# First graph loop: ScalarE fetches a second tile of every twelfth superstep row by row

## Chip, cores and metric

One core of one Trainium2 chip runs the kernel. The metric is the device time of one execution in microseconds, as the median of the runs.

## What is computed

Two graph layers over 12500 nodes with 64 features and 200000 edges, sorted by destination. Each layer is followed by a residual and a layer norm. The reference, cut to what matters:

```python
# layer 0
all_feat = concat([x[dst], x[src], edge_attr, u_per_node[dst]])
msg = relu(all_feat @ W1 + b1)
agg = segment_sum(msg, dst, num_segments=12500)
x = layernorm(x + relu(concat([x, agg, u_per_node]) @ W2 + b2))
# layer 1: relational attention, 8 relations
Z = einsum('ni,rio->nro', x, fc_weight)
z_s, z_d = Z[src, etype], Z[dst, etype]
e = relu(sum(concat([z_s, z_d]) * attn_weight[etype]))
alpha = exp(e - segment_max(e)[dst]) / segment_sum(...)[dst]
x = layernorm(x + segment_sum(alpha * z_s, dst))
```

## The kernel before

**Tiling.** The edges lie in NT = 1563 tiles of 128 edges. O = 8 tiles make a superstep of the table, of which there are TO = 196. A tile whose edges go to two blocks of 128 nodes is worked on twice, so the consuming engines run SO = 208 supersteps of eight slots. Superstep s of the consumers needs the table up to a superstep that they read from a row of numbers (`xrow`); it is at most s + 1 supersteps and lags behind s more and more, 12 in the end.

**The first loop** (`phase_layer0`) adds up the messages of layer 0. In it,

- GpSimd (POOL) gathers: `gathers` issues one indirect DMA for each tile (line 522). It reads 128 rows of 64 floats of `Btab` (x[src] times its weights, made beforehand) into the tile `ring`. The ring has RT = 20 supersteps of the table, and three spare ones of eight tiles. At the first tile of superstep s >= 20 it waits for `full` of consumer superstep s - 20 + 13 (`BEHIND` = 13), and at tiles 2, 4 and 6 for sums before that. After the fourth tile of superstep s, `counted(s - 1)` (line 510) waits for the DMAs of superstep s - 1 and raises `landed` by one.
- SyncE (SP) issues for each consumer superstep the load of `eaT` (edge features, line 636), which waits for TensorE's count `c` (line 635), and every fourth the load `drow` (line 534). Beside it `fetched` (lines 476 to 496) fetches the last tile (j = 7) of every twelfth superstep of the table, 17, 29, ... (NK = 15 tiles), one row after another, by 128 small DMAs with a row number from a register. It spreads them over twelve consumer supersteps, 11 rows (`ROWS`) in each. `numbers` (line 473) loads the 128 row numbers of the next such tile. POOL leaves these 15 tiles out, and `counted` waits for their rows too (`s_row`). For k = 0 the rows are issued in consumer supersteps 0 to 11, and `counted(17)` asks for them.
- TensorE (PE) multiplies A3 by the one-hot `oht` (line 791), and `eaT` (line 796), and then sums the messages by destination (line 804).
- VectorE (DVE) makes the one-hot tiles (902, 906), adds the three parts (945), adds the gathered rows of `ring` (`full`, line 925, which waits for `landed`), then adds slot by slot into `p_t` (931), and adds the sums into `acc0` (918).
- ScalarE (ACT) does one thing in each of the 208 supersteps: it waits for `pre` and writes `msg` = relu of `p_t` (line 704). PE's sums of the superstep and DVE's next line 945 wait for it. Before the loop it zeroes `acc0` (line 701).

**Around it.** Each phase is a block that all engines end together. `phase_mid` computes x1 and `Ztab`, and `phase_layer1` is a second loop of the same shape with POOL gathering from `Ztab`, SP fetching 15 tiles by rows, and ACT busy with two sets of activations in each superstep. The edge source numbers come from `in_srcT_in`, or from `srcT_s` where the edges had to be sorted first; SP has one copy of its loop for each case.

Of the kernel before, what the change touches and what calls it, by code (L numbers as in the profile page):

```python
# [13 lines left out]
P = 128  # L14
# [44 lines left out]
class Chain:  # L59


    def __init__(self, e, sem):
        self.e, self.sem = e, sem
# [401 lines left out]
def fetched_tile(k):  # L465


    return (FIRST + k * W) * O + O - 1


def numbers(e, A, of, k):

    e.dma_start(A.srow[0:1, k % 2 * P:(k % 2 + 1) * P], of[:, fetched_tile(k):fetched_tile(k) + 1].rearrange("p c -> c p"),
                allow_slow_non_contiguous=True).then_inc(A.s_srow, 16)


def fetched(e, A, s, ring, table, of, regs, used):


    k, i = divmod(s, W)  # L480
    if k >= NK:
        return
    t = fetched_tile(k)
    if i == 0:
        if k >= 2:

            e.wait_ge(used, t // O - SPARE * W + BEHIND + 1)
            e.wait_ge(A.s_row[k % 2], 16 * P * (k // 2))
        e.wait_ge(A.s_srow, 16 * (k + 1))
        if k + 1 < NK:  # L490
            numbers(e, A, of, k + 1)
    for p in range(i * ROWS, min((i + 1) * ROWS, P)):
        if p % O == 0 or p == i * ROWS:
            e.reg_load(regs, A.srow[0:1, k % 2 * P + p // O * O:k % 2 * P + p // O * O + O])
        r = e.snap(regs[p % O], min_val=0, max_val=table.shape[0] - 1)
        e.dma_start(ring[p:p + 1, place(t), :], table[bass.ds(r, 1), :]).then_inc(A.s_row[k % 2], 16)


def gathers(e, A, ring, table, idx, s_g, landed, used, summed, free={}):

    others = {fetched_tile(k): k for k in range(NK)}
# [3 lines left out]
    def counted(s):  # L505
        e.wait_ge(s_g[s % len(s_g)], 16 * sum(tiles(i) for i in range(s % len(s_g), s + 1, len(s_g))))
        k = others.get(s * O + O - 1)
        if k is not None:
            e.wait_ge(A.s_row[k % 2], 16 * P * (k // 2 + 1))
        e.sem_inc(landed, 1)  # L510
# [27 lines left out]
def phase_layer0(nc, A):  # L538
# [3 lines left out]
    with ExitStack() as ctx:  # L542
# [51 lines left out]
        s_io = sem("l0_io")  # L594
        T = {n: sem("t_" + n) for n in ("dve count before middle low high typ val sq sel tab d0 rows rowt rowi table dh dl lt yt ys "
# [4 lines left out]
        def _(e):  # L600
# [21 lines left out]
            def loads(of, src):  # L622
                numbers(e, A, src, 0)
                for s in range(SO):
# [12 lines left out]
                    fetched(e, A, s, ring, A.Btab, src, regs, S["full"])  # L637
# [7 lines left out]
        @block.gpsimd  # L645
        def _(e):
            gathers(e, A, ring, A.Btab, idx, s_g, S["landed"], S["full"], S["acc"], {XT0 // O: (T["a"], len(CHUNKS))})

        @block.scalar
        def _(e):  # L650
# [50 lines left out]
            e.activation(A.acc0, A.ones[:, 0:D].unsqueeze(1).to_broadcast([P, NB + 1, D]), ACT.Copy, scale=0.0).then_inc(T["zero"], 1)  # L701
            for s in range(SO):
                e.wait_ge(S["pre"], s + 1)
                e.activation(msg[:, s % 2, :, :], pT[:, :, :], ACT.Relu).then_inc(S["msg"], 1)  # L704

# [254 lines left out]
def phase_mid(nc, A):  # L960
# [6 lines left out]
    with ExitStack() as ctx:  # L967
# [31 lines left out]
        s_zd = [sem(f"mid_zd{i}") for i in range(ZR)]  # L999
        s_ix = sem("mid_ix")  # L1000
# [302 lines left out]
def phase_layer1(nc, A):  # L1303

    QO, QT, QV = 5, 3, 4
    with ExitStack() as ctx:
# [39 lines left out]
        def _(e):  # L1346
            numbers(e, A, A.ix1_d, 0)
            regs = [e.alloc_register(f"l1sr{j}") for j in range(O)]
            for s in range(SO):
                if s % G == 0:  # L1350
                    rows_loaded(e, A, drow, s_dr, S["oht"], s // G)
                fetched(e, A, s, ring, A.Ztab, A.ix1_d, regs, S["s"])
            e.wait_ge(A.s_srow, 16 * NK)

        @block.gpsimd
        def _(e):
            gathers(e, A, ring, A.Ztab, idx, s_g, S["landed"], S["s"], S["acc"])
# [300 lines left out]
def build(nc, A):  # L1658
    with ExitStack() as ctx:
# [28 lines left out]
        A.srow = A.tabs[96:97, 0:2 * P]  # L1688

        A.s_row = [ctx.enter_context(nc.semaphore(f"rows_fetched{i}")) for i in range(2)]  # L1690
        A.s_srow = ctx.enter_context(nc.semaphore("row_numbers"))

# [91 lines left out]
```

## Time and profile before

| what | value |
|---|---|
| time, median of 3 runs | 5698.01 us (5693.83 to 5705.06) |
| span of the profiled execution | 4163.5 us |
| time less span | 1534.5 us |
| first loop, POOL's first gather to the end of the block | 36.1 to 2005.6 us of the span |
| PE, DVE, POOL busy | 78%, 72%, 72% of the span |
| ACT busy | 31% of the span |
| mean granted TensorE clock | 0.522 of full speed |

The profiled execution shows its span from the first to the last instruction, and no time of its own beside it, so the difference of 1534.5 us is between that span and the median of other executions. Busy shares don't count DMA issues, register work or waits: POOL at 72% can be at work without a break, since a gather's record covers only part of the distance to the next gather. `POOLq`, `SPq` and `ACTq` are the sequencers of these engines.

### The profile page before, as it was taken

The numbers are of one execution on the slowest core, as the hardware profiler recorded it, in microseconds if no ns is written. First come the engines' busy times: TensorE is split into PE (matmuls) and PEld (weight loads), VectorE is DVE, ScalarE is ACT, GpSimd is POOL, SyncE is SP. The second block draws the span as 40 slices with busy tenths as digits, with TensorE's granted clock in tenths as the row PEclk, the third lists the DMA queues.
The fourth block names the chain that finished last, engine by engine and source line by source line (L and its number), as shares of the span: only waits on it lengthen the run. The fifth ranks groups of instructions, "written<-read, shape, count | busy, mean of one in ns | idle before, by whom it ended". The sixth has DMA issues, their size and how long they took to land. (4 is left out here: it accounts for less than half of the span.)

```text
span 4163.5 us, 83378 instructions
## 1 busy us (share of the span) xinstructions
PE 3242.3 (78%) x17947; PEld 2881.6 (69%) x17947; DVE 2994.8 (72%) x9502; ACT 1276.9 (31%) x4180; POOL 3008.4 (72%) x3234
## 2 busy tenths in 40 slices
PE   7887777777777777777857787788888888888885
PEld 6776666676667676767637676777777777777774
DVE  6776676677777777777656666676767777777777
ACT  3000000000000000000334555455555555555555
POOL 5777777777777777777257777777777777777773
PEclk7555555555555555555675555555555555555555
DMA  5322222222222222222352122222222222222221
GB/s 185 104 74 71 72 61 72 70 73 62 72 72 73 72 73 62 75 69 63 140 211 60 49 59 60 60 60 49 59 60 52 56 59 51 58 59 69 49 59 38
DMA packets 183679, 300.98 MB, mean 72 GB/s; under 512 B 83240, under 2 KB 89756, under 8 KB 169885
## 3 DMA queue, kind: packets, MB, share of 16 engines
q1 hardware_dynamic: 82662, 189.29, 12.9%
q0 software_dynamic: 99072, 104.03, 11.9%
q8 instruction: 173, 2.83, 0.3%
q14 instruction: 310, 2.53, 0.2%
q10 hardware_dynamic: 1462, 2.30, 0.2%
HBM read 260.38 MB, written 34.99 MB: 71 GB/s over the span
## 5 line engine op out<-in xcount | busy, mean ns | idle before, releaser
L522 POOL DMA_INDIRECT ring<-Btab,idx x1548 | 1473.7, 952 | 505.0 <-issue 325.8
L522 POOL DMA_INDIRECT ring<-Ztab,idx x1548 | 1469.3, 949 | 481.3 <-issue 345.8
L1423 PE MATMUL p_s<-ring,ohx 128*128 x3328 | 809.8, 422 | 159.2 <-issue 156.6
L1423 PEld LDWEIGHTS p_s<-ring,ohx 128*128 128x128 f32 x3328 | 737.5, 326 | 179.3 <-issue 179.3
L804 PEld LDWEIGHTS p_s<-msg,oh 128*128 128x128 f32 x3328 | 726.0, 330 | 97.8 <-issue 97.6
L804 PE MATMUL p_s<-msg,oh 128*128 128x64 f32 x3328 | 756.6, 422 | 46.8 <-ACT msg L704 44.0
L791 PE MATMUL p_m<-A,oht 128*128 x1664 | 435.8, 364 | 394.1 <-DVE full L925 384.7
L704 ACT ACTIVATE msg<-p_t 128x512 f32<-128x512 f32 x208 | 124.2, 597 | 1786.6 <-DVE p_t L931 1786.6
L796 PE MATMUL p_m<-W1c,eaT 65*128 65x128 f32 x1664 | 574.3, 449 | 26.2 <-DMA eaT<-in_eaT_in 26.1
L791 PEld LDWEIGHTS p_m<-A,oht 128*128 128x128 bf16 x1664 | 233.2, 140 | 472.1 <-issue 426.0
L1511 DVE SCALAR_TENSOR_TENSOR XA<-XA,ff,p_s 128x65 f32 x1664 | 467.9, 281 | 127.7 <-DVE XA L1511 71.3
L1374 ACT ACTIVATE ohe<-oh,ev 128x128 f32<-128x128 bf16 x1664 | 505.1, 386 | 31.2 <-DVE ev L1471 31.2
L1368 ACT ACTIVATE ohx<-oh,ex 128x128 f32<-128x128 bf16 x1664 | 508.6, 388 | 0.0
L796 PEld LDWEIGHTS p_m<-W1c,eaT 65*128 65x128 f32 x1664 | 455.2, 334 | 37.0 <-DMA eaT<-in_eaT_in 30.9
L1402 PE MATMUL p_ei<-ring,ident_h 128*128 x1664 | 320.4, 197 | 193.5 <-POOLq L510 189.3
L925 DVE TENSOR_TENSOR full<-p_m,ring 128x512 f32 x208 | 143.4, 690 | 429.2 <-POOLq L510 415.7
L1408 PE MATMUL p_x<-ident,ohe 128*128 128x128 f32 x1664 | 397.5, 417 | 0.0
L931 DVE TENSOR_TENSOR p_t<-p_t,full 128x64 f32<-128x64 f32 x1664 | 386.1, 233 | 12.1 <-issue 6.6
L918 DVE TENSOR_TENSOR XA<-XA,p_s 128x64 f32 x1664 | 366.7, 220 | 35.5 <-issue 7.5
L945 DVE TENSOR_REDUCE p_t<-p_m 128x256 f32<-128x768 f32 x416 | 379.2, 954 | 17.2 <-PE p_m L796 16.6
L1402 PEld LDWEIGHTS p_ei<-ring,ident_h 128*128 128x128 bf16 x1664 | 173.3, 106 | 299.1 <-issue 228.4
L1481 DVE TENSOR_REDUCE mslot<-p_x 128x8 f32<-128x1024 f32 x208 | 254.7, 1224 | 160.6 <-PE p_x L1408 159.8
(225 smaller groups left out, 3114.3 us busy)
## 6 DMA issues: line engine op xcount, KB each, us to landing
drow<-drow_d SPq DMA_DIRECT2D x104, 1024.0 KB
ring<-Btab SPq DMA_DIRECT2D x1920, 0.2 KB
ring<-Ztab SPq DMA_DIRECT2D x1920, 0.3 KB
eaT<-in_eaT_in SPq DMA_DIRECT2D x208, 128.0 KB
Ztab<-Z_stage SPq DMA_DIRECT2D x49, 536.0 KB, 5.2
ring<-Btab,idx POOLq DMA_INDIRECT x1548
ring<-Ztab,idx POOLq DMA_INDIRECT x1548
xTB<-in_xTB_in SPq DMA_DIRECT2D x7, 448.0 KB, 7.7
```

Of the source, the lines that this page charges most:

```text
L522: e.indirect_dma_start(out=ring[:, place(t), :], out_offset=None, in_=table[:, :], in_offset=bass.IndirectOffsetOnAxis(ap=idx[:, t:t + 1], ...
L791: e.matmul(parts(j), OHT[:, s % 2, j, :], A.A3[:, bass.ds(b, 1), :].rearrange("p a c -> p (a c)"), start=True, stop=True)
L796: last = e.matmul(own(j // 2), eaT[:, s % QE, j // 2, :], A.W1c2[:, :], start=True, stop=True)
L804: last = e.matmul(pS[r % 2][:, j, :], OH[:, r % QO, j, :], msg[:, r % 2, j, :], start=True, stop=True)
L931: ins = e.tensor_tensor(out=pT[:, j:j + 1, :], in0=pT[:, j:j + 1, :], in1=full[:, bass.ds(t, 1), :], op=ALU.add)
L945: e.tensor_reduce(out=pT[:, h * H:(h + 1) * H, :], in_=half(h), axis=AXX, op=ALU.add).then_inc(T["dve"], 1)
L1368: ins = e.activation(OHx[:, o, j, :], OH[:, s % QO, j, :], ACT.Copy, scale=ex[:, o, j:j + 1])
L1374: ins = e.activation(OHe[:, s % 2, j, :], OH[:, s % QO, j, :], ACT.Relu, scale=ev[:, s % QV, j:j + 1])
L1402: last = e.matmul(pE[:, j, :], A.ident_h[:, :], part.unsqueeze(2).to_broadcast([P, 3, R]), start=False, stop=True)
L1408: last = e.transpose(pX[:, j, :], OHe[:, s % 2, j, :], A.ident[:, :])
L1423: last = e.matmul(pS[s % 2][h][:, j % 4, :], OHx[:, s % 2, j, :], ring[:, bass.ds(t, 1), 0:D + 1], start=True, stop=True)
L1511: e.scalar_tensor_tensor(out=acc, in0=acc, scalar=ff[:, s % QV, j:j + 1], in1=pS[s % 2][j // 4][:, j % 4:j % 4 + 1, :], op0=ALU.mult, op1= ...
```

## The change

`fetched_tile` becomes a class `Rows` that holds which tile of the twelfth superstep is meant (`back`), where its numbers lie and its semaphores. SP keeps its tile (j = 7). In the first loop alone ACT gets a second one (`by_act`, `back` = 2, that is j = 6 of supersteps 17, 29, ...): after each relu it issues 11 row DMAs, with its own semaphores and numbers. Before its loop it writes the source numbers to a new array `srcT_d` and loads the first 128 numbers from there, so that it needs one copy of the loop alone. POOL leaves both tiles out, 30 in all where it left out 15, and `counted` waits for both. At its end ACT takes its semaphores back to zero, and `phase_mid` uses them again. The second loop stays with SP alone.

```diff
--- before.py
+++ after.py
@@ -462,51 +462,57 @@
     return RING + n % SPARE * O + j if off == 0 and n >= 0 else t % RING
 
 
-def fetched_tile(k):
-
-
-    return (FIRST + k * W) * O + O - 1
-
-
-def numbers(e, A, of, k):
-
-    e.dma_start(A.srow[0:1, k % 2 * P:(k % 2 + 1) * P], of[:, fetched_tile(k):fetched_tile(k) + 1].rearrange("p c -> c p"),
-                allow_slow_non_contiguous=True).then_inc(A.s_srow, 16)
-
-
-def fetched(e, A, s, ring, table, of, regs, used):
+class Rows:
+
+
+    def __init__(self, back, numbers, s_numbers, s_rows, before=0):
+        self.back, self.numbers, self.s_numbers, self.s_rows, self.before = back, numbers, s_numbers, s_rows, before
+
+    def tile(self, k):
+        return (FIRST + k * W) * O + O - self.back
+
+
+def numbers(e, rows, of, k):
+
+    t = rows.tile(k)
+    e.dma_start(rows.numbers[0:1, k % 2 * P:(k % 2 + 1) * P], of[:, t:t + 1].rearrange("p c -> c p"),
+                allow_slow_non_contiguous=True).then_inc(rows.s_numbers, 16)
+
+
+def fetched(e, rows, s, ring, table, of, regs, used):
 
 
     k, i = divmod(s, W)
     if k >= NK:
         return
-    t = fetched_tile(k)
+    t = rows.tile(k)
     if i == 0:
         if k >= 2:
 
             e.wait_ge(used, t // O - SPARE * W + BEHIND + 1)
-            e.wait_ge(A.s_row[k % 2], 16 * P * (k // 2))
-        e.wait_ge(A.s_srow, 16 * (k + 1))
+            e.wait_ge(rows.s_rows[k % 2], 16 * P * (k // 2))
+        e.wait_ge(rows.s_numbers, 16 * (k + 1 + rows.before))
         if k + 1 < NK:
-            numbers(e, A, of, k + 1)
+            numbers(e, rows, of, k + 1)
     for p in range(i * ROWS, min((i + 1) * ROWS, P)):
         if p % O == 0 or p == i * ROWS:
-            e.reg_load(regs, A.srow[0:1, k % 2 * P + p // O * O:k % 2 * P + p // O * O + O])
+            e.reg_load(regs, rows.numbers[0:1, k % 2 * P + p // O * O:k % 2 * P + p // O * O + O])
         r = e.snap(regs[p % O], min_val=0, max_val=table.shape[0] - 1)
-        e.dma_start(ring[p:p + 1, place(t), :], table[bass.ds(r, 1), :]).then_inc(A.s_row[k % 2], 16)
-
-
-def gathers(e, A, ring, table, idx, s_g, landed, used, summed, free={}):
-
-    others = {fetched_tile(k): k for k in range(NK)}
+        e.dma_start(ring[p:p + 1, place(t), :], table[bass.ds(r, 1), :]).then_inc(rows.s_rows[k % 2], 16)
+
+
+def gathers(e, A, ring, table, idx, s_g, landed, used, summed, fetchers, free={}):
+
+    others = {rows.tile(k) for rows in fetchers for k in range(NK)}
     tiles = lambda s: sum(t < NT and t not in others for t in range(s * O, (s + 1) * O))
 
 
     def counted(s):
         e.wait_ge(s_g[s % len(s_g)], 16 * sum(tiles(i) for i in range(s % len(s_g), s + 1, len(s_g))))
-        k = others.get(s * O + O - 1)
-        if k is not None:
-            e.wait_ge(A.s_row[k % 2], 16 * P * (k // 2 + 1))
+        k, off = divmod(s - FIRST, W)
+        if off == 0 and 0 <= k < NK:
+            for rows in fetchers:
+                e.wait_ge(rows.s_rows[k % 2], 16 * P * (k // 2 + 1))
         e.sem_inc(landed, 1)
 
     for t in range(NT):
@@ -592,6 +598,7 @@
         s_ea = [sem(f"l0_ea{q}") for q in range(QE)]
         s_dr = [sem(f"l0_dr{q}") for q in range(2)]
         s_io = sem("l0_io")
+        by_act = Rows(2, A.arow, A.s_arow, A.s_arows, 1)
         T = {n: sem("t_" + n) for n in ("dve count before middle low high typ val sq sel tab d0 rows rowt rowi table dh dl lt yt ys "
                                         "drow typd ix a hi lo rem parts zero").split()}
         block = ctx.enter_context(nc.Block())
@@ -620,7 +627,7 @@
             rows_loaded(e, A, drow, s_dr, S["oht"], 0)
 
             def loads(of, src):
-                numbers(e, A, src, 0)
+                numbers(e, A.by_sp, src, 0)
                 for s in range(SO):
                     if s == 4:
 
@@ -634,7 +641,7 @@
                         e.wait_ge(S["c"], s - QE + 1)
                     t = e.snap(treg, min_val=1, max_val=TO)
                     e.dma_start(eaT[0:2 * DE, s % QE, :, :], of[bass.ds(t, 1), :, :, :].rearrange("a f i k -> (a f) i k")).then_inc(s_ea[s % QE], 16)
-                    fetched(e, A, s, ring, A.Btab, src, regs, S["full"])
+                    fetched(e, A.by_sp, s, ring, A.Btab, src, regs, S["full"])
 
             bad = descends(e, A, "l0_sp")
             with e.If(bad == 0):
@@ -644,7 +651,7 @@
 
         @block.gpsimd
         def _(e):
-            gathers(e, A, ring, A.Btab, idx, s_g, S["landed"], S["full"], S["acc"], {XT0 // O: (T["a"], len(CHUNKS))})
+            gathers(e, A, ring, A.Btab, idx, s_g, S["landed"], S["full"], S["acc"], [A.by_sp, by_act], {XT0 // O: (T["a"], len(CHUNKS))})
 
         @block.scalar
         def _(e):
@@ -699,9 +706,20 @@
             e.wait_ge(T["drow"], 16)
             e.wait_ge(T["typd"], 32)
             e.activation(A.acc0, A.ones[:, 0:D].unsqueeze(1).to_broadcast([P, NB + 1, D]), ACT.Copy, scale=0.0).then_inc(T["zero"], 1)
+            e.dma_start(A.srcT_d, idx[:, :]).then_inc(A.s_arow, 16)
+
+            regs = [e.alloc_register(f"l0ar{j}") for j in range(O)]
+
+            e.wait_ge(A.s_arow, 16)
+            numbers(e, by_act, A.srcT_d, 0)
             for s in range(SO):
                 e.wait_ge(S["pre"], s + 1)
                 e.activation(msg[:, s % 2, :, :], pT[:, :, :], ACT.Relu).then_inc(S["msg"], 1)
+                fetched(e, by_act, s, ring, A.Btab, A.srcT_d, regs, S["full"])
+
+            for k in range(2):
+                take(e, A.s_arows[k], 16 * P * len(range(k, NK, 2)))
+            take(e, A.s_arow, 16 * (NK + 1))
 
         @block.tensor
         def _(e):
@@ -996,8 +1014,8 @@
             "b2 turned copied w2 o1 ln sub sq var root x1").split())
         s_ps, s_se, s_pp, s_zp, s_z, s_zv, s_za, s_cont, s_v = (sem("mid_" + n) for n in (
             "s s_copied parts zparts z zv za cont pool").split())
-        s_zd = [sem(f"mid_zd{i}") for i in range(ZR)]
-        s_ix = sem("mid_ix")
+        s_zd = A.s_arows + [sem(f"mid_zd{i}") for i in range(2, ZR)]
+        s_ix = A.s_arow
         block = ctx.enter_context(nc.Block())
         Zv = A.Ztab.rearrange("(b p r) c -> p b (r c)", p=P, r=R)
         blocks = lambda i: slice(i * LNB, (i + 1) * LNB)
@@ -1344,17 +1362,17 @@
 
         @block.sync
         def _(e):
-            numbers(e, A, A.ix1_d, 0)
+            numbers(e, A.by_sp, A.ix1_d, 0)
             regs = [e.alloc_register(f"l1sr{j}") for j in range(O)]
             for s in range(SO):
                 if s % G == 0:
                     rows_loaded(e, A, drow, s_dr, S["oht"], s // G)
-                fetched(e, A, s, ring, A.Ztab, A.ix1_d, regs, S["s"])
+                fetched(e, A.by_sp, s, ring, A.Ztab, A.ix1_d, regs, S["s"])
             e.wait_ge(A.s_srow, 16 * NK)
 
         @block.gpsimd
         def _(e):
-            gathers(e, A, ring, A.Ztab, idx, s_g, S["landed"], S["s"], S["acc"])
+            gathers(e, A, ring, A.Ztab, idx, s_g, S["landed"], S["s"], S["acc"], [A.by_sp])
 
         @block.scalar
         def _(e):
@@ -1686,9 +1704,14 @@
         A.wrow = A.tabs[32:33, :].rearrange("a (s j) -> a s j", j=O)
         A.xrow = A.tabs[64:65, 0:SO * WX].rearrange("a (s w) -> a s w", w=WX)
         A.srow = A.tabs[96:97, 0:2 * P]
+        A.arow = A.tabs[96:97, 2 * P:4 * P]
 
         A.s_row = [ctx.enter_context(nc.semaphore(f"rows_fetched{i}")) for i in range(2)]
         A.s_srow = ctx.enter_context(nc.semaphore("row_numbers"))
+        A.by_sp = Rows(1, A.srow, A.s_srow, A.s_row)
+
+        A.s_arows = [ctx.enter_context(nc.semaphore(f"act_rows{i}")) for i in range(2)]
+        A.s_arow = ctx.enter_context(nc.semaphore("act_row_numbers"))
 
         A.dstl = sb("dstl", [P, NS], BF16)
 
@@ -1769,6 +1792,7 @@
     A.typ_s = dr("typ_s", (SCP * P,), I32)
     A.srcT_s = dr("srcT_s", (P, NTP), I32)
     A.typT_s = dr("typT_s", (P, NTP), I32)
+    A.srcT_d = dr("srcT_d", (P, NTP), I32)
     A.ea_s = dr("ea_s", (EP, DE), F32)
     A.eaT_s = dr("eaT_s", (TO + 1, 2 * DE, O // 2, P), F32)
     A.drow_d = dr("drow_d", (NS, P), BF16)
```

## Rows read from the trace of the kernel before

**Rows 1.** The page: the span, and busy time, share and count of each engine.

```profile
span 4163.5 us, 83378 instructions
PE 3242.3 (78%) x17947; PEld 2881.6 (69%) x17947; DVE 2994.8 (72%) x9502; ACT 1276.9 (31%) x4180; POOL 3008.4 (72%) x3234
```

**Rows 2.** The page's costliest groups: busy, mean of one, idle before and its releaser.

```profile
L522 POOL DMA_INDIRECT ring<-Btab,idx x1548 | 1473.7, 952 | 505.0 <-issue 325.8
L704 ACT ACTIVATE msg<-p_t 128x512 f32<-128x512 f32 x208 | 124.2, 597 | 1786.6 <-DVE p_t L931 1786.6
L925 DVE TENSOR_TENSOR full<-p_m,ring 128x512 f32 x208 | 143.4, 690 | 429.2 <-POOLq L510 415.7
```

**Rows 3.** Windows of the loop, with and without SP's rows: length, then busy (xcount).

```profile
130.00:1730.00 1600.00, 1219.24 (x5572) 1101.89 (x5573) 1190.05 (x3644) 103.28 (x173) 1210.34 (x1279) 0.50 0.24 70
1760.00:1980.00 220.00, 167.66 (x769) 151.99 (x768) 164.53 (x505) 14.33 (x24) 166.50 (x176) 0.50 0.24 65
```

**Rows 4.** Timeline mid-loop: start, length, instruction, idle before and releaser.

```profile
...
1002.95 0.94 POOL L522 DMA_INDIRECT ring<-Btab,idx  x1 [0.30 <-issue]
...
1004.20 0.94 POOL L522 DMA_INDIRECT ring<-Btab,idx  x1 [0.30 <-issue]
...
1008.09 0.69 DVE L925 TENSOR_TENSOR full<-p_m,ring 128x512 f32 x1 [2.94 <-POOLq L510]
...
1011.86 0.60 ACT L704 ACTIVATE msg<-p_t 128x512 f32<-128x512 f32 x1 [9.35 <-DVE p_t L931]
...
1019.14 0.60 ACT L704 ACTIVATE msg<-p_t 128x512 f32<-128x512 f32 x1 [6.69 <-DVE p_t L931]
...
1026.03 0.60 ACT L704 ACTIVATE msg<-p_t 128x512 f32<-128x512 f32 x1 [6.29 <-DVE p_t L931]
...
```

**Rows 5.** Timeline at the start of the first loop, POOL and ACT.

```profile
...
36.13 1.13 POOL L522 DMA_INDIRECT ring<-Btab,idx  x1 [33.14 <-POOLq L309]
...
81.79 5.48 ACT L701 ACTIVATE XA<-ones 128x6336 f32<-128x6336 f32 x1
93.63 0.60 ACT L704 ACTIVATE msg<-p_t 128x512 f32<-128x512 f32 x1 [6.35 <-DVE p_t L931]
```

**Rows 6.** Timeline: relu of supersteps 11 and 13, gathers of tiles 147 and 160.

```profile
...
190.68 0.60 ACT L704 ACTIVATE msg<-p_t 128x512 f32<-128x512 f32 x1 [6.47 <-DVE p_t L931]
...
205.67 0.60 ACT L704 ACTIVATE msg<-p_t 128x512 f32<-128x512 f32 x1 [6.30 <-DVE p_t L931]
...
225.80 0.94 POOL L522 DMA_INDIRECT ring<-Btab,idx  x1 [0.30 <-issue]
...
242.03 0.94 POOL L522 DMA_INDIRECT ring<-Btab,idx  x1 [0.30 <-DVE full L925]
```

**Rows 7.** Timeline at the end of the first loop, POOL and ACT.

```profile
...
1980.68 0.94 POOL L522 DMA_INDIRECT ring<-Btab,idx  x1 [0.30 <-DVE XA L918]
...
1997.47 0.60 ACT L704 ACTIVATE msg<-p_t 128x512 f32<-128x512 f32 x1 [6.39 <-DVE p_t L931]
...
2005.56 0.27 POOL L1244 MEMSET Z_stage<- 128x96 f32 x1 [23.93 <-POOLq L542]
```

**Rows 8.** SP's own waits: who waited for whom, us in total, times, longest.

```profile
SPq L635 <- PEq L802: 506.5, 161, 11.0
```

**Rows 9.** Timeline of SP in supersteps 1 and 2.

```profile
...
90.47 0.53 SPq L636 DMA_DIRECT2D eaT<-in_eaT_in  x1
91.73 5.20 SPq L496 DMA_DIRECT2D ring<-Btab  x11
97.67 0.49 SPq L636 DMA_DIRECT2D eaT<-in_eaT_in  x1
```

**Rows 10.** Line 496, one row DMA: count, ns min/median/max.

```profile
...
L496 SPq DMA_DIRECT2D ring<-Btab x1920: 219/225/322, 84.4 to 1737.9; - x192
```

**Rows 11.** Timeline: the same kind of load issued by SP and by ACT.

```profile
...
2005.57 2.11 SPq L1277 DMA_DIRECT2D xT<-in_xTA_in  x4
...
2005.98 2.03 ACTq L1099 DMA_DIRECT2D xT<-in_xTA_in  x3
```


## Prediction

> **What bounds the kernel now.** I read the page first. Its span is 4163.5 us and no engine is busy for more than 78% of it [rows 1], so busy shares don't name the bound. The costliest groups do. For the first loop they show 1548 indirect gathers on POOL, a mean of 952 ns each, with 505.0 us idle before them, or 0.33 us each [rows 2]. Is that idle time a wait? In the timeline two gathers start at 1002.95 and 1004.20 us: 0.94 us of work and 0.30 us put down to "issue", which is the same before every gather [rows 4]. The table of windows says it for the whole loop: 1279 gathers in 1600 us, 1.251 us each (its columns are busy times, POOL's the last of the five, with the count in brackets) [rows 3]. POOL is never stopped; 505.0 less 1548 x 0.30 less the 33.1 us before the first gather [rows 2, 5] leaves nothing to speak of. Those who wait are the others: DVE's line 925 waits 415.7 us for POOL's sequencer, and ACT waits 1786.6 us of the loop for DVE [rows 2]. Where DVE has its rows already it makes a superstep in 1026.03 - 1019.14 = 6.89 us [rows 4]; POOL needs 1548 x 1.251 / 208 = 9.31 us for one on average. So **POOL's count of gathers sets the first loop**, from 36.1 us to its last gather at 1980.7, with 24.9 us behind it to the end of the block, which is the other engines' last supersteps at their own pace [rows 5, 7].
>
> **The sum.** POOL loses 15 gathers of 1.251 us: 15 x 1.251 = 18.8 us. Its waits stay: the change adds one in `counted`, 15 times, beside the one for SP's rows; the next gathers are queued behind it, and DVE waits for `landed`, so it matters only if ACT's rows are late (next paragraph). The end of the loop moves with POOL's last gather, since the supersteps behind it carry no row fetches (the 15 tiles are issued in supersteps 0 to 179 of 208) and keep their 24.9 us [rows 7]. `phase_mid` and the second loop only start earlier. The span becomes 4163.5 - 18.8 = 4144.7 us. The time of 5698.0 us has 1534.5 us around the span, which no row explains; I hold it constant: **5698.0 - 18.8 = 5679.2 us**.
>
> **Are ACT's rows in time for POOL?** For the first tile (superstep 17) ACT issues its last rows after the relu of superstep 11, at 190.7 us; `counted(17)` comes with the gather of tile 147 at 225.8 us, now 1.3 us earlier [rows 6]. Between them lie 34 us, for some 7 us of issuing and a landing. Later tiles have more: ACT's superstep 12k + 11 against POOL's 12k + 18, where both go at POOL's pace. The other wait of POOL, for `full` of superstep 13 at tile 160, is met about 205.7 us and asked for at 242.0 [rows 6]: 36 us for any slowing of DVE.
>
> **What ACT pays.** 1920 row DMAs, 195 or so register loads, 15 number loads. The trace has no such work on ACT; the nearest is SP's. SP goes from `eaT`'s issue to the next in 97.67 - 90.47 = 7.20 us; of that 5.20 us are 11 rows, 0.473 each, and 0.73 us lie between `eaT`'s end and the first row [rows 9]. With those prices ACT needs 0.60 + 0.73 + 5.20 = 6.5 us in a superstep, under even DVE's 6.89. ACT may issue more slowly: of the same kind of load SP issues four in 2.11 us, 0.53 each, and ACT three in 2.03, 0.68 each [rows 11]. A row at 0.473 x 0.68/0.53 = 0.61 us gives 0.60 + 0.73 + 6.7 = 8.0 us. That delays the relu in the short supersteps by 1.1 us, and with it PE's line 804 and DVE's 945, which wait for `msg`; but the mean superstep is still POOL's 1533 x 1.251 / 208 = 9.22 us, and the delay goes into DVE's wait for POOL. At the start of the loop it adds up over some 14 supersteps to 15 us, inside the 34 and 36 us above. So I cost it at nothing, between nothing and rival 1; a gain is excluded, as ACT's relu gets no earlier.
> From which price does it count? relu 0 is at 93.6, relu 207 at 1997.5 us [rows 5, 7], and the last 27 supersteps at 6.9 take 187 us, so supersteps 0 to 179 have 1717 us; less some 15 for the one stall among them (rival 1) it is 9.5 each. ACT reaches that at (9.5 - 1.33)/11 = 0.74 us a row, SP at 0.473 + (9.5 - 7.2)/11 = 0.68.
>
> **What comes before the loop.** ACT writes `srcT_d` (784 KB), waits for it, and loads 128 numbers. Zeroing `acc0` ends at 87.3 us and the first relu starts at 93.6, 6.35 us idle [rows 5]. If it doesn't fit, the first supersteps slip by a few us, and POOL, at work since 36.1 us, has the same 34 us of room.
>
> **The descriptor hardware.** A row DMA is recorded with 225 ns, under half of its 473 ns [rows 9, 10]. If only those 225 ns exclude the other queue, two streams need 450 ns of each 473 and both fit, barely. If each row waits in full for one of the other's, it costs 225 ns more. The Trainium skill speaks for the second: "Perfetto Trace Analysis", section on the HWDGE DMA instruction, says that the two sequencers share one descriptor generator, locked for exclusive use, and that the reported time includes the wait for the lock. By this rule the sum would be rival 1's. That two queues issue at once with 0.53 and 0.68 us a load [rows 11] shows no doubling.
>
> **The rivals.**
> 1. **SP becomes the bound, slower.** Place: SP's eleven rows, with the next `eaT` queued behind them, for which PE waits. Price: each row waits 0.225 us for one of ACT's, SP's superstep is 7.20 + 11 x 0.225 = 9.7 us. Then relu 207 comes at 93.6 + 180 x 9.7 + 187 + about 15 us (the stall in supersteps 3 and 4, where SP's queue holds the load of x) = 2042 instead of 1997.5: +44 us, 5742. It decides from 0.68 us a row on. For it: the 450 of 473 ns. Against it: SP today waits 506.5 us in the loop for PE [rows 8], which is 2.4 us a superstep, and ACT issues in only part of SP's time. Chance 9%.
> 2. **The gathers get dearer and nothing is gained.** 18.8 / 1533 = 0.012 us more for each gather, 1%, would eat it all: 5698. POOL writes its descriptors while ACT's transfers run. Against it: with SP's rows 1600/1279 = 1.251, without them 220/176 = 1.250 us [rows 3]; one stream of rows costs 1 ns at most. This case also holds that the fetched tiles don't lie where POOL is bound. Chance 10%.
> 3. **The time around the span grows with the program.** It is 1534.5 us over 83378 recorded instructions [rows 1], 18 ns each. The change adds at least 2 x 1920 and some for the registers, about 4100: +75 us, 5698 - 19 + 75 = 5754. No row supports a charge per instruction. Chance 5%.
> 4. **It shrinks with POOL's gathers.** 1534.5 / 3096 gathers = 0.50 us each, 15 x 0.50 = 7 us more saved: 5672. Chance 5%.
> The Trainium skill ("Runtime: NRT & Kernel Launch", its section on the preamble and postamble) gives a launch about 15 us; 1534.5 us here is a hundred times that, so the page doesn't explain it, and I take nothing from it.
>
> **How the numbers follow.** Forecast 71%, rivals 9, 10, 5 and 5%. The likeliest time is 5679.2. The runs shown lie 11 us apart, so a median may be off by some 4 us; the forecast alone is 5674 to 5685. The range takes in rival 4 (5672 less 4) and rival 2 (5698 and some): 5668 to 5702, and leaves out rivals 1 and 3, 14%. About 0.2%, or 11.4 us, is what a measurement of this kernel can tell from no change: faster means below 5686.6. The forecast is 7 us under that; of its 71% I give 66 to faster and 5 to same. Faster: 66 + 5 = 71%; same: 5 + 10 = 15%; slower: 14%.
>
> **What would show it.** In the trace after: 1533 gathers from `Btab`, still 1.25 us from start to start, and no new wait on POOL; POOL's last gather near 1962 us; the second loop as long as before. ACT's row DMAs at 0.47 to 0.61 us apart and its relu at least 6.5 us apart; SP's rows still near 0.47. The window without row fetches should look as before. I am wrong if SP's or ACT's rows stand over 0.7 us apart, if POOL's gathers start more than 1.26 us apart, if DVE's line 925 no longer waits for POOL, or if the span falls by 19 us and the time does not.

## The result, and the profile after

| | before | after | ratio, 95% interval |
|---|---|---|---|
| beside the timed runs shown ahead of the prediction | 5703.1 us (5693.8 to 5715.9) | 5769.9 us (5732.5 to 5785.9) | 1.0102 [1.0080, 1.0123] |
| on another chip (e5) | 4159.6 us (4152.5 to 4162.2) | 4140.0 us (4133.6 to 4144.9) | 0.9955 [0.9941, 0.9968] |

The forecast was 5679.2 us. The change made the kernel 1.0% slower where it was timed. On another chip it made the same kernel 0.45% faster. The kernel before takes 5.70 to 5.78 ms on some chips and 4.16 ms on others, always the same kind for all executions on one chip, and the trace shown ahead of the prediction (span 4163.5 us) is of the second kind while the times beside it are of the first.

The page of the changed kernel where it was timed. The rows with digits are busy tenths in 40 slices, PEclk is the granted TensorE clock; in the groups the columns are busy, mean ns, and idle before with its releaser. "issue" there means that the profile shows nothing the engine still waited for, "remote" that it can't name what raised the semaphore. The lines have moved: 528 is the gather (522 before), 717 the relu (704), 814 and 822 PE's `eaT` and its sums (796, 804), 936 DVE's sums into `acc0` (918), 943 `full` (925), 949 the additions into `p_t` (931), 963 the three parts (945).

```profile
...
span 5730.8 us, 89576 instructions
...
PE 3325.5 (58%) x17947; PEld 2864.8 (50%) x17947; DVE 3013.2 (53%) x9502; ACT 1277.1 (22%) x4180; POOL 2987.0 (52%) x3219
...
PE   4164544544454454555685076666666667666676
...
DVE  3264454545454455555684065555555555555567
...
POOL 4525555555555555555405616666666666666641
PEclk9999999999999999999997555555555555555555
...
L528 POOL DMA_INDIRECT ring<-Btab,idx x1533 | 1456.3, 950 | 1368.6 <-DVE XA L936 761.5
...
L814 PE MATMUL p_m<-W1c,eaT 65*128 65x128 f32 x1664 | 589.6, 458 | 735.2 <-DMA eaT<-in_eaT_in 641.3
...
L717 ACT ACTIVATE msg<-p_t 128x512 f32<-128x512 f32 x208 | 124.2, 597 | 2683.1 <-issue 1803.0
L963 DVE TENSOR_REDUCE p_t<-p_m 128x256 f32<-128x768 f32 x416 | 391.9, 962 | 613.1 <-remote 397.4
```

The span is 5730.8 us where [rows 1] had 4163.5, and that execution took 5732.5 us: 1.7 us around the span, not 1534.5. The first loop fills slices 2 to 21 (a slice is 143 us); from its first relu to its last are 2794 us, in place of 1904. POOL, without a break in [rows 2], has 1368.6 us of idle time before its gathers, 761.5 of it for DVE's sums, and its mean gather still takes 950 ns. PE waits 641.3 us for `eaT` from SP, ACT stands 2683.1 us. Nobody is the plain bound. Two of the prediction's signs of being wrong are there: DVE's line 943 no longer waits for POOL (before it, 200.3 us of "issue" and nothing else), and SP's rows stand 0.74 us apart at the median (0.42 in e5).

The same kernel on the other chip (e5), where the kernel before has the rows of the first trace again:

```profile
...
span 4134.9 us, 89576 instructions
...
PE 3230.8 (78%) x17947; PEld 2874.3 (70%) x17947; DVE 2995.2 (72%) x9502; ACT 1276.8 (31%) x4180; POOL 2987.8 (72%) x3219
...
L528 POOL DMA_INDIRECT ring<-Btab,idx x1533 | 1454.2, 949 | 501.1 <-issue 345.2
...
L717 ACT ACTIVATE msg<-p_t 128x512 f32<-128x512 f32 x208 | 124.2, 597 | 1768.9 <-DVE p_t L949 1747.9
...
L943 DVE TENSOR_TENSOR full<-p_m,ring 128x512 f32 x208 | 143.6, 690 | 408.4 <-POOLq L516 396.4
```

Here all reads as in [rows 1, 2]: 1533 gathers, 501.1 us idle before them, DVE waiting 396.4 us for POOL.

### The profile page after: what moved, and what is told of

Same layout as the page of the kernel before. It is cut to its first block and busy times, and to the rows that moved or that the text cites. A ratio compares the mean times of both kernels' runs of the same rounds, so it can differ in the third digit from the quotient of the medians.

```text
span 5730.8 us, 89576 instructions
## 1 busy us (share of the span) xinstructions
PE 3325.5 (58%) x17947; PEld 2864.8 (50%) x17947; DVE 3013.2 (53%) x9502; ACT 1277.1 (22%) x4180; POOL 2987.0 (52%) x3219
## 5 line engine op out<-in xcount | busy, mean ns | idle before, releaser
L528 POOL DMA_INDIRECT ring<-Btab,idx x1533 | 1456.3, 950 | 1368.6 <-DVE XA L936 761.5
L814 PE MATMUL p_m<-W1c,eaT 65*128 65x128 f32 x1664 | 589.6, 458 | 735.2 <-DMA eaT<-in_eaT_in 641.3
L822 PE MATMUL p_s<-msg,oh 128*128 128x64 f32 x3328 | 742.3, 417 | 167.2 <-ACT msg L717 143.6
L717 ACT ACTIVATE msg<-p_t 128x512 f32<-128x512 f32 x208 | 124.2, 597 | 2683.1 <-issue 1803.0
L963 DVE TENSOR_REDUCE p_t<-p_m 128x256 f32<-128x768 f32 x416 | 391.9, 962 | 613.1 <-remote 397.4
L1415 PE MATMUL p_ei<-S,oht 128*128 x1664 | 325.1, 199 | 607.2 <-issue 517.2
L1415 PEld LDWEIGHTS p_ei<-S,oht 128*128 128x128 bf16 x1664 | 174.3, 105 | 723.1 <-issue 676.1
L1535 DVE TENSOR_REDUCE md<-p_b 128x8 f32<-128x24 f32 x208 | 38.0, 183 | 857.4 <-remote 824.7
L920 DVE TENSOR_TENSOR oh<-p_i,dstl 128x1024 f32<-128x1024 f32 x208 | 253.2, 1217 | 437.4 <-remote 437.1
L1426 PE MATMUL p_x<-ident,ohe 128*128 128x128 f32 x1664 | 429.2, 416 | 74.1 <-issue 73.4
L1426 PEld LDWEIGHTS p_x<-ident,ohe 128*128 128x128 f32 x1664 | 345.0, 234 | 119.2 <-issue 118.0
```

The lines of the kernel that those rows point to most:

```text
L528: e.indirect_dma_start(out=ring[:, place(t), :], out_offset=None, in_=table[:, :], in_offset=bass.IndirectOffsetOnAxis(ap=idx[:, t:t + 1], ...
L814: last = e.matmul(own(j // 2), eaT[:, s % QE, j // 2, :], A.W1c2[:, :], start=True, stop=True)
L822: last = e.matmul(pS[r % 2][:, j, :], OH[:, r % QO, j, :], msg[:, r % 2, j, :], start=True, stop=True)
L963: e.tensor_reduce(out=pT[:, h * H:(h + 1) * H, :], in_=half(h), axis=AXX, op=ALU.add).then_inc(T["dve"], 1)
L1415: e.matmul(pE[:, j, :], OHT[:, s % QT, j, :], A.S23[:, bass.ds(b, 1), :], start=True, stop=False)
L1426: last = e.transpose(pX[:, j, :], OHe[:, s % 2, j, :], A.ident[:, :])
```

## Experiments

**Two kinds of chips.** Each paragraph says which kind the kernels met: "4.16 ms" or "5.7 ms" is the time of the kernel before there. Theory A1 below is the prediction's.

**e1, the kernel before again (4.16 ms).**

> The unchanged kernel, for a trace of an execution that takes as long as the timed ones (5.70 ms), since the trace first shown had a span of only 4163.5 us. Theory A, that SyncE's sequencer stalls in such executions: SyncE's own register and DMA instructions show stretches at 0.70 us or a multiple for each, as the trace of the changed kernel does (1995 of them over 0.64 us), TensorE waits hundreds of us for eaT, the span is within 5 us of 5700. Theory B, that the missing 1534 us lie outside the span: the span is again near 4163 us.

4161.1 us, span 4159.3. What it asked for, a trace of a 5.7 ms execution, it didn't give. It showed that the first trace was no odd one: this kernel has executions of 4.16 ms, and 1.8 us lie around their span. Theory B fell.

**e2, e4: no rows in the first loop; in no loop (4.16 ms).** Base: the changed kernel. What only the rows need goes too, among it ACT's copy to `srcT_d`; the cut shows the main lines.

```diff
-                numbers(e, A.by_sp, src, 0)
...
-                    fetched(e, A.by_sp, s, ring, A.Btab, src, regs, S["full"])
...
-            numbers(e, by_act, A.srcT_d, 0)
-                fetched(e, by_act, s, ring, A.Btab, A.srcT_d, regs, S["full"])
-            gathers(..., [A.by_sp, by_act], ...)
+            gathers(..., [], ...)
```

(e4 takes the same out of the second loop.)

> Nobody fetches by rows in the first loop; POOL gathers all 1563 tiles. The second loop is unchanged. Theory A (the sequencers that issue rows are the bound): the first loop goes to POOL's pace, 1563 x 1.25 us and 25 us behind it, so it ends near 2020 us instead of near 3000, and the time falls to 4700 to 4900 us. Theory B (POOL's count of gathers is the bound): 15 x 1.25 = 19 us slower than before, 5717 us.

> Nobody fetches by rows in either loop; POOL gathers 1563 tiles in each. Theory A: both loops at POOL's pace, near 4163 + 30 x 1.25 = 4200 us. Theory B: 38 us slower than before, 5736 us.

e2: 4179.1 us against 4159.4, 1.0047 [1.0031, 1.0064], 19.8 us for 15 more gathers, 1.32 us each. e4: 4195.4 us, 1.0091 [1.0074, 1.0108], 36.0 us for 30, 1.20 each. That is the price from [rows 3], 1.251, from both sides: on this kind of chip both loops go by POOL's count.

**e3, ScalarE's rows alone (4.16 ms).** e2 with ACT's stream kept.

> In the first loop ScalarE alone fetches its 15 tiles by rows, SyncE none; POOL gathers as many tiles as in the kernel before. Theory A with the stall tied to how much a sequencer issues: SyncE is free, eaT comes in time, but ScalarE's rows hold up the relu as SyncE's held up eaT: between e2 and before, 4900 to 5600 us. If only the sum of both streams were too much: near e2. Theory B: as before, 5700 us.

4167.8 us, 1.0026 [1.0013, 1.0039]; again in e12 4162.5 us, 1.0007 [0.9998, 1.0017]. The gathers are as many as before. The 8.4 us that e3 is over didn't come back in e12 (4.4 us), so it makes little difference whose rows spare them.

**e5, the changed kernel (4.16 ms).**

> The changed kernel beside the kernel before on one chip, with both in executions of the same kind. If the kernel before takes 4.16 ms here (as beside e1 to e4): theory A1, POOL's count of gathers sets the loop and ScalarE's rows are hidden: 4159.4 - 18.8 = 4140.6 us. Theory A2, every row stream costs something by itself, as e3 came out 8.4 us over before with the same number of gathers: 4140.6 + 8 = 4149 us. Theory C, the loss of 1% is a property of the kernel at any speed: 1.01 x 4159 = 4201 us. If the kernel before takes 5.7 ms: 5765 us by all of them.

4140.0 us, 0.9955 [0.9941, 0.9968]: 19.6 us less, where the sum said 18.8. Windows of its first loop, with and without rows (busy by engine, count in brackets):

```profile
...
130.00:1730.00 1600.00, 1234.83 (x5645) 1116.19 (x5644) 1207.94 (x3698) 105.11 (x176) 1209.90 (x1280) 0.50 0.27 72
1760.00:1957.00 197.00, 153.07 (x702) 138.83 (x701) 149.39 (x459) 13.13 (x22) 149.16 (x158) 0.50 0.25 63
```

POOL: 1600/1280 = 1.250 us, 197/158 = 1.247 us a gather, as in [rows 3]; two streams of rows beside it cost it nothing. ACT in the middle of the loop:

```profile
...
902.06 0.60 ACT L717 ACTIVATE msg<-p_t 128x512 f32<-128x512 f32 x1 [9.69 <-DVE p_t L949]
902.96 5.52 ACTq L501 DMA_DIRECT2D ring<-Btab  x11
911.86 0.60 ACT L717 ACTIVATE msg<-p_t 128x512 f32<-128x512 f32 x1 [9.20 <-DVE p_t L949]
912.75 7.06 ACTq L501 DMA_DIRECT2D ring<-Btab  x11
```

Eleven rows in 5.52 us, 0.50 each, and the next relu 3.4 us after them. Some supersteps need 7 us. What ACT's relu waited for in this execution, and SP's wait for PE:

```profile
...
  DVE p_t L949: 1747.9, 205
  DMA ring<-Btab: 14.0, 2
  issue: 7.0, 1
```

```profile
...
SPq L642 <- PEq L820: 482.9, 156, 10.5
```

Three relus of 208, all before 400 us, are put down to ACT's own DMAs or to "issue"; the 14.0 and 7.0 us are the whole idle time before them, most of which was there anyway: the relu never starts over 1.0 us behind DVE's last addition. SP waits 482.9 us where [rows 8] had 506.5: its rows are not slower for ACT's. Theories A2 and C fell.

**e6, e10, e13: ScalarE's stream by itself.** ACT's rows go to a tile that nobody reads, POOL gathers as in the kernel before.

```diff
...
+        aside = sb("aside", [P, 2, D], F32)
...
-                fetched(e, by_act, s, ring, A.Btab, A.srcT_d, regs, S["full"])
+                fetched(e, by_act, s, aside, A.Btab, A.srcT_d, regs, S["full"], lambda k: k % 2)
-            gathers(..., [A.by_sp, by_act], ...)
+            gathers(..., [A.by_sp], ...)
```

> The changed kernel, but ScalarE's rows go to a tile of their own that nobody reads, and POOL gathers that tile too, so that POOL has as many gathers as before: the price of ScalarE's stream by itself. At 4.16 ms: theory A1 4159 us, no change; theory A2 4168 us, 8 more. At 5.7 ms: the whole loss and the gain that is not taken, 5765 + 19 = 5784 us, if ScalarE's stream holds up the loop.

> The same kernel as e6, to be read on a chip where the kernel before takes 5.7 ms. Theory L (each row adds its share to what SyncE and ScalarE have to get through in POOL's pauses; from e7 and the changed kernel's own result: 0.07 us a row on SyncE, 0.04 on ScalarE, a gather 1.25 us): 1920 x 0.04 = 76 us over the kernel before, about 5790 us. If the loss were in the second loop or outside the first: the same as before, 5716 us. If the chip is of the 4.16 ms kind: 4159 us again, no change.

> The same kernel as e6 and e10, for a chip where the kernel before takes 5.7 ms. There, theory L: 76 us over the kernel before, about 5790 us. If the loss of the changed kernel is not ScalarE's rows: 5716 us. On a chip of the 4.16 ms kind: 4159 us.

At 4.16 ms: 1.0002 [0.9992, 1.0011] and 1.0004 [0.9994, 1.0013], nothing at all. At 5.7 ms (e13): 5888.5 us against 5772.5, **1.0202 [1.0172, 1.0232]**, 116 us slower, 0.06 us for each of 1920 rows. This is the loss, shown by itself: on a chip of this kind, ACT's stream costs 2%. It lies in the first loop: from its first relu to its last e13 takes 2896 us and e18 (below, the kernel before on another chip of the kind) 2785. The changed kernel's loss of 1.0%, 67 us, was measured on another chip; the 49 us between the two would be what the 15 spared gathers give back, over twice their 18.8 us, and no run on one chip shows that share.

**e7, about half the rows (5.7 ms).** The changed kernel with W = 24 in place of 12, for both loops: 21 tiles are fetched by rows where it fetches 45, and the kernel before 30.

> The changed kernel with the fetched tiles in every twenty-fourth superstep, in both loops: SyncE and ScalarE issue 6 rows a superstep in place of 11; POOL gathers 1549 and 1556 tiles (before: 1548 and 1548), 9 more than before and 23 more than the changed kernel. Executions of 4.16 ms, POOL's count alone: 9 x 1.25 = 11 us over the kernel before. Executions of 5.7 ms: theory S (instructions of SyncE and ScalarE wait 0.70 us each while POOL gathers without a break, so a superstep takes POOL's 9.3 us and the rows' own 5): about 2.5 us less in each of 180 supersteps and in both loops, 4.8 to 5.2 ms. Theory T (these executions are slow whatever is issued): within 1% of the kernel before.

5601.3 us against 5716.7, 0.9798 [0.9772, 0.9823]. Fewer rows help, by 115 us against the kernel before and not by the 500 to 900 of theory S. `eaT` is in time now: PE waits 0.6 us for it, 641.3 in the timed trace. Its first loop still takes 13.6 us a superstep from relu to relu (changed kernel: 14.1; the first trace 9.2), and 13.4 us between supersteps 168 and 188, where no row is issued. So the rows, and `eaT` that is late behind them, add to these executions and don't make them.

**e8, e9: dearer rows on ScalarE, on SyncE (5.7 ms).** The row numbers are loaded again before every second row, in the first loop, by ACT alone in e8 and by SP alone in e9.

```diff
-        if p % O == 0 or p == i * ROWS:
+        if p % O == 0 or p == i * ROWS or (rows.reload and p % 2 == 0):
```

> The changed kernel with the row numbers loaded again before every second row on ScalarE (six loads of about 0.79 us a superstep in place of about two): a row there costs some 0.8 us. Executions of 4.16 ms: the sum's threshold of 0.74 us a row on ScalarE is passed, its superstep is 0.6 + 0.1 + 11 x 0.82 = 9.7 us, so 180 supersteps at 9.7 in place of 9.12: 104 us slower than the changed kernel, 4245 us (4160 to 4330). If ScalarE's rows were hidden at any price: 4140 us.

> The same on SyncE in the first loop, ScalarE as in the changed kernel. SyncE's superstep is 0.5 + 0.7 + 0.1 + 9.0 = 10.3 us: 180 x (10.3 - 9.12) = 212 us slower than the changed kernel, 4350 us (4250 to 4450). If eaT is loaded early enough for SyncE to lag without harm: 4140 us.

e8: 5982.4 us, 1.0465 [1.039, 1.0541]; e9: 5860.9, 1.0253 [1.0217, 1.0289]. The kernel before took 5716.7 here. They met the other kind of chip, so the sum's thresholds (0.74 and 0.68 us a row) stay untested. What they say is that work on ACT's sequencer costs more than the same on SP's: taking the changed kernel at its +1.0%, which was measured on another chip, 207 against 86 us; the 121 us between e8 and e9 are of one chip. In e8 ACT's relu starts over 0.5 us after DVE's last addition in 159 supersteps of 208, in e9 in 6.

**e11, e12: no rows, ScalarE's rows alone (4.16 ms).**

> The same kernel as e4. On a chip of the 5.7 ms kind, theory L: 3840 x 0.07 = 280 us less for the rows, 38 more for the gathers, about 5475 us. Theory S (a superstep takes POOL's time and the rows' on top, the rows are what makes these executions slow): 4.2 to 4.8 ms. If the rows cost nothing there: 5716 + 38 = 5754 us. On a chip of the 4.16 ms kind: 4196 us again.

> The same kernel as e3. On a chip of the 5.7 ms kind, theory L: 1920 x (0.07 - 0.04) = 60 us less than before, about 5655 us. If ScalarE's rows are the dearer ones, as its relu stands in the chain of every superstep: over 5716 us. On a chip of the 4.16 ms kind: 4160 to 4168 us.

They met the 4.16 ms kind: e11 4197.1 us, 1.0090 [1.0074, 1.0107], as e4.

**e14: no rows in either loop (5.7 ms).**

> The same kernel as e4 and e11. On a chip of the 5.7 ms kind, theory L: about 5475 us; theory S: 4.2 to 4.8 ms; rows free: 5754 us. On a chip of the 4.16 ms kind: 4196 us.

5616.5 us against 5772.5, **0.9724 [0.9699, 0.9749]**, 156 us faster, with 30 gathers more. Theory S fell for good: 5.6 ms without a single row. Theory L had the sign and the wrong size (156 us where it wanted 240, and 116 in e13 where it wanted 76). On this kind of chip this kernel beats both; on the other it is the slowest of the three.

**e16, e17: meant to set POOL's gathers apart.** Base: the kernel before. e16 has two memsets behind each gather of the first loop, e17 two register loads.

> The kernel before with two small memsets on POOL behind each gather of the first loop, so that gathers start some 1.5 us apart in place of 1.25. On a chip of the 4.16 ms kind POOL is the bound: 1548 x 0.25 = 390 us slower, some 4550 us. On a chip of the 5.7 ms kind, theory P: with at most seven gathers in any 10 us the others get through, a superstep takes 7.44 x 1.5 = 11.2 us in place of 14, 400 to 500 us faster, near 5250 us. If the stalls don't come from how closely POOL's gathers follow each other: no faster than before.

> The kernel before with two register loads on POOL's sequencer behind each gather of the first loop, to set the gathers some 1.6 us apart (e16's memsets fitted into the 0.30 us between two gathers and left them at 1.25). On a chip of the 4.16 ms kind POOL is the bound: 1548 x 0.35 = 540 us slower, 4500 to 4900 us. On a chip of the 5.7 ms kind, theory P: at most six or seven gathers in any 10 us, the others get through, a superstep takes 7.44 x 1.6 = 12 us in place of 14, 200 to 400 us faster than before. If the stalls don't come from how closely POOL's gathers follow each other: as before or slower.

Neither set them apart. e16 (4.16 ms): 4161.8 us, 1.0005. The memsets lie in the gap and the gathers still start 1.25 us apart:

```profile
...
1000.30 0.12 POOL L525 MEMSET spacer<- 128x1 bf16 x1
1000.33 0.12 POOL L526 MEMSET spacer<- 128x1 bf16 x1
1000.61 0.94 POOL L522 DMA_INDIRECT ring<-Btab,idx  x1 [0.16 <-issue]
1001.55 0.12 POOL L525 MEMSET spacer<- 128x1 bf16 x1
```

e17 (5.7 ms): 5780.6 us, 1.0005 [0.9992, 1.0018]; its trace has the same 83378 instructions as e18's, no register loads behind POOL's gathers, and gathers at 1.25 us, so the loads, whose values nobody used, were not in the program that ran. Theory P was not tested by either.

**e15, e18: the trace of the kernel before.**

> The kernel before, unchanged, for its trace on a chip of the 5.7 ms kind: there, theory P (SyncE's and ScalarE's instructions wait while POOL gathers back to back) wants SyncE's register instructions at 0.70 us after eight gathers in 10 us and none after few, a superstep of the first loop near 14.0 us with rows (changed kernel 14.1), and POOL waiting for the sums of DVE. On a chip of the 4.16 ms kind: a superstep at 9.23 us as in e1.

> The kernel before, for its trace on a chip of the 5.7 ms kind: a superstep of the first loop at 14.0 us, SyncE's register instructions at 0.70 us after eight gathers in 10 us and none after few. On a chip of the 4.16 ms kind: 9.23 us a superstep, as in e1 and e15.

e15 met the 4.16 ms kind (4163.5 us, as e1). e18 gave the trace that was missing when I predicted, 5773.7 us:

```profile
...
span 5772.0 us, 83378 instructions
...
L522 POOL DMA_INDIRECT ring<-Btab,idx x1548 | 1467.7, 948 | 1348.5 <-DVE XA L918 725.6
...
L796 PE MATMUL p_m<-W1c,eaT 65*128 65x128 f32 x1664 | 589.6, 458 | 657.4 <-DMA eaT<-in_eaT_in 591.4
...
L704 ACT ACTIVATE msg<-p_t 128x512 f32<-128x512 f32 x208 | 124.2, 597 | 2673.5 <-issue 1417.1
```

This is the page to predict from for a time of 5700 us. POOL is no bound (1348.5 us idle before its gathers, not 505.0 [rows 2]), PE waits 591.4 us for `eaT`. From relu to relu 14.07 us in supersteps 0 to 180, where the first trace has 9.23. Where do they go? Line 496 on SP, with min/median/max in ns, here and in e1:

```profile
...
L496 SPq MOVE ring<-Btab x1920: 2/29/1407, 146.5 to 2678.6; - x192
L496 SPq DMA_DIRECT2D ring<-Btab x1920: 2/225/1409, 146.6 to 2679.3; - x192
```

```profile
...
L496 SPq MOVE ring<-Btab x1920: 29/29/38, 82.4 to 1735.4; - x192
L496 SPq DMA_DIRECT2D ring<-Btab x1920: 219/225/322, 82.5 to 1735.5; - x192
```

A MOVE is a register instruction of 29 ns. Here it takes up to 1407. In the trace as recorded, with starts and lengths of every instruction, SP and ACT then advance in step, one instruction each 0.70 us, or each 1.40 us when both are at it (changed kernel, where it was timed; start, end in us, length in ns):

```
1659.51  1660.20  694  Sync    FUSED_REGOPS
1659.53  1660.22  694  Scalar  MOVE
1660.90  1661.60  700  Sync    MOVE
1660.92  1661.62  700  Scalar  DMA_DIRECT2D
1662.30  1663.00  700  Sync    DMA_DIRECT2D
1662.32  1663.02  700  Scalar  FUSED_REGOPS
1663.70  1664.40  700  Sync    FUSED_REGOPS
```

SP's rows in e18 and POOL's gathers beside them:

```profile
...
1605.21 4.88 SPq L496 DMA_DIRECT2D ring<-Btab  x11
1610.87 0.49 SPq L636 DMA_DIRECT2D eaT<-in_eaT_in  x1
1612.11 10.75 SPq L496 DMA_DIRECT2D ring<-Btab  x11
```

```profile
...
1601.14 0.94 POOL L522 DMA_INDIRECT ring<-Btab,idx  x1 [0.30 <-issue]
1610.35 0.94 POOL L522 DMA_INDIRECT ring<-Btab,idx  x1 [8.27 <-DVE XA L918]
1611.59 0.94 POOL L522 DMA_INDIRECT ring<-Btab,idx  x1 [0.30 <-issue]
...
1619.08 0.94 POOL L522 DMA_INDIRECT ring<-Btab,idx  x1 [0.30 <-issue]
1623.67 0.94 POOL L522 DMA_INDIRECT ring<-Btab,idx  x1 [3.64 <-DVE XA L918]
```

Eleven rows take 4.88 us when POOL paused before, and 10.75 us when POOL gathered through them. Counting the register and semaphore instructions of SP and ACT from 200 to 2600 us (register loads, long by themselves, left out) by how many gathers started in the 10 us before, the share of them that took over 0.64 us:

```
gathers before   0     2     4     6     7     8
e18, before     1%    1%    8%   12%   39%   76%
after           0%    1%    4%    9%   45%   81%
```

And the stretch of e18 with POOL's gathers against the one behind its last gather (the third pair is DVE, the fifth POOL):

```profile
...
400.00:2600.00 2200.00, 1116.55 (x5056) 1003.78 (x5056) 1103.51 (x3316) 93.73 (x157) 1183.14 (x1250) 1.00 0.18 48
2820.00:2950.00 130.00, 123.92 (x578) 114.72 (x577) 123.10 (x387) 11.34 (x19) 0.00 (x0) 1.00 0.13 43
```

DVE is busy for 1103.5 of 2200 us with POOL at work and 123.1 of 130 without. The last 14 supersteps, behind POOL's last gather, take 6.9 to 7.3 us each. The stalls are not confined to SP and ACT, and it isn't their rows that bring them. In e14, without a row, none of the 162 such instructions of SP and ACT after eight gathers took over 0.64 us, but 69 of DVE's 119 did (DVE in e18: 21%, in the changed kernel: 41%). And TensorE stands between two matmuls for which the profile shows no wait, while POOL gathers every 1.25 us:

```profile
...
1513.85 3.01 PE L810 MATMUL p_s<-msg,oh 128*128 128x64 f32 x13 [0.39 <-ACT msg L709]
1517.19 0.27 PE L810 MATMUL p_s<-msg,oh 128*128 128x64 f32 x1 [0.34 <-issue]
1520.01 0.27 PE L810 MATMUL p_s<-msg,oh 128*128 128x64 f32 x1 [2.56 <-issue]
1522.12 0.27 PE L810 MATMUL p_s<-msg,oh 128*128 128x64 f32 x1 [1.85 <-issue]
```

Such idle time before this line is 495.1 us in e14 and nothing in e4, the same kernel at 4.16 ms. So on this kind of chip PE and DVE lose time directly, with or without rows, and this fits e14's 5.6 ms; SP's and ACT's part comes on top. In e18 and the changed kernel the stalls go with POOL's gathers. That POOL's gathers cause them is argued from this and not shown by an experiment, and why one chip has them and another not is open.

## Why the prediction was wrong

1. **The bound.** "POOL's count of gathers sets the first loop" is true of the execution whose trace I read: e2, e4 and e5 give 1.32, 1.20 and 1.31 us a gather for 1.251. It is false of the executions that were timed. There POOL waits 725.6 us of the loop for DVE's sums (e18).
2. **The step that failed** is "The time of 5698.0 us has 1534.5 us around the span, which no row explains; I hold it constant". In each of the 19 executions profiled since, of either kind, 1.7 to 1.8 us lie around the span. So the 1534.5 us lay inside the loops of other executions, and a difference that no row explains, a quarter of the time, said that the trace and the times were not of one kind. Rivals 3 and 4 looked at those 1534.5 us too, and both kept them outside. The rival that was missing: the timed executions are bound by something else, and there the rows that I cost at nothing have a price.
3. **What ACT pays**, "I cost it at nothing". Right at 4.16 ms (1.0002 and 1.0004; in the lines of e5 a row takes 0.50 to 0.64 us, where the estimate had 0.47 to 0.61). Wrong at 5.7 ms: 116 us. The sum let the delay of the relu go "into DVE's wait for POOL"; that wait was 415.7 us in [rows 2] and is not there in e18, so a delay has nothing to go into. One way of the loss is the one that the sum named: ACT's sequencer holds the relu behind its rows. ACT's relu in the timed trace of the changed kernel, and in e14 without rows:

```profile
...
  issue: 1803.0, 133
  DVE p_t L949: 746.6, 67
  DMA ring<-Btab: 133.5, 8
```

```profile
...
  issue: 2083.4, 144
  DVE p_t L937: 500.4, 64
```

133.5 us of waits for the rows' DMAs are there in one and not in the other; "issue" holds the rest, which the profile can't divide. From DVE's last addition to the relu, the timed trace has 42 supersteps with over 0.5 us, 351 us together, and e13 has 42, 325 us together; e18 and e14 have none. Of this only a part reaches PE: before its sums it waits for `msg` 143.6 us in the timed trace and 62.2 in e13, where e18 has 17.3. The other way is `eaT` (point 4), and how the 116 us divide between the two no run shows.
4. **Rival 1**, SP becomes the bound: at 4.16 ms nothing of it (482.9 us of SP's wait left). At 5.7 ms SP is late for `eaT` even before the change (e18: 591.4 us of PE's waits), and with ACT's stream later still. In e13:

```profile
...
POOL ring L528 <- DVE XA L937: 850.3, 142, 13.7
...
PE p_m L815 <- DMA eaT<-in_eaT_in: 746.1, 151, 17.0
```

746.1 us for `eaT` and 850.3 us of POOL waiting for DVE, where e18 has 591.4 and 725.6 (other chips of the kind). This rival named the place, SP's late `eaT`, but for the descriptor hardware as its reason; e6 shows that it is not that, since two streams at 4.16 ms cost nothing. That its 5742 us and rival 3's 5754 came nearer to the 5769.9 measured than the forecast is luck. The lock that the Trainium skill describes ("Perfetto Trace Analysis", the section on the HWDGE DMA instruction) leaves no mark in e5: line 501's row DMA on SP has a median of 225 ns, as in [rows 10], with ACT's at 230 beside it, and ACT's is 230 in e3 too, where SP issues no rows in the first loop.
5. **Rows in time for POOL, the start of the loop, the end:** right. First relu at 92.6 us in e5 (93.6), last gather near 1957 (the sum wanted 1962), no new wait on POOL.
6. **Rival 2**, dearer gathers: no, 1.250 and 1.247 us. **Rivals 3 and 4**: no, with 1.7 to 1.8 us around every span nothing there grows or shrinks by tens of us. Rival 3 also took 4100 more instructions, and the pages show 6198 (89576 for 83378).

## What to carry to other kernels

Before a sum is made, the span of the profiled execution must explain the timed one; where it leaves out more than a few us, the profile is of another kind of execution and its bound is not the bound of the times. Work moved from the engine that seems to be the bound to an idle sequencer is free only while that sequencer keeps its pace: a small stream beside the one instruction in the chain (the relu) cost 0% on two chips and 2% on a third. A change of 0.4% should be measured on more than one chip before it is kept.

## What was not expected of the hardware

- One program takes 4.16 ms on some chips and 5.7 ms on others: four comparisons of each kind stand here, with the kernel before at 4158 to 4161 us on the ones and 5703 to 5780 on the others.
- On the slow kind, after eight gathers of POOL in 10 us, 76 to 81% of SP's and ACT's register and semaphore instructions take over 0.64 us (e18, changed kernel), many of them 0.70, in turn between the two. DVE and PE stall too, even where SP and ACT fetch no rows: PE loses 495.1 us before one line in e14 and nothing in e4. POOL's own pace stays 1.25 us a gather, and a matmul that runs keeps its length (line 804: 422 ns in the first trace, line 822: 417 ns in the changed kernel's).
- The granted TensorE clock is 1.0 of full speed (2.4 GHz) through the first loop there, and 0.5 (1.2 GHz) in the first trace, where PE is busy for 78% in place of 58%. So the slower executions have the higher clock there. It is not what makes them slow: in the second loop it is 0.50 in e18 (3200 to 5300 us) and 0.51 in e1 (2300 to 3700 us), and SP's rows of that loop run over 2341 us in e18 and 1661 in e1.
- 0.30 us between two gathers on POOL hold two small memsets for nothing (e16).
